# Causal attention in a decoder kernel: sums by quads of key tiles, a staggered search, and rows kept on chip

## What is computed

```python
scores = jnp.einsum('bhqd,bhkd->bhqk', q, k) * scale
scores = jnp.where(causal, scores, jnp.finfo(jnp.float32).min)
ex = jnp.exp(scores - jnp.max(scores, axis=-1, keepdims=True))
attn = ex / (jnp.sum(ex, axis=-1, keepdims=True) + 1e-08)
o = jnp.einsum('bhqk,bhkd->bhqd', attn, v)
out = jnp.einsum('bsi,oi->bso', o.transpose(0, 2, 1, 3).reshape(B, S, D), w_out) + b_out
```

## Time and profile before

| what | value |
|---|---|
| median of 3 runs | 9607.21 us (9586.43 to 9630.57) |
| profiled execution | 9610.03 us, its span 9608.2 us |
| PE busy | 7068.8 us, 74% of the span |
| DVE busy | 6895.6 us, 72% |
| ACT busy | 4456.8 us, 46% |
| POOL busy | 3936.4 us, 41% |
| mean granted PE clock | 0.748 of full speed |

### The profile page before, as it was taken

How to read it: one execution, slowest core, us unless ns; L and a number is a source line. 1 busy time by engine, 2 the same in 40 slices (tenths; PEclk the granted TensorE clock), 3 DMA queues, 4 the chain that set the end, 5 groups by cost and what they waited for, 6 DMA issues and landing times. The chain is left out here.

```text
span 9608.2 us, 163672 instructions
## 1 busy us (share of the span) xinstructions
PE 7068.8 (74%) x30924; PEld 2767.1 (29%) x30924; DVE 6895.6 (72%) x47725; ACT 4456.8 (46%) x8379; POOL 3936.4 (41%) x2613
## 2 busy tenths in 40 slices
PE   6888557666667656899766766656656789999983
PEld 2222222222222223555322222222223322222222
DVE  2655279999999997455399999999998343343423
ACT  1444246666666554111266767657656422222220
POOL 1000035555555443122155556545555045555550
PEclk7889656666666655799766677766766899999986
DMA  1000200000000000000100000000000311111103
GB/s 58 25 22 19 39 15 7 5 7 8 5 8 5 8 4 2 20 20 13 36 5 5 9 5 9 5 8 5 9 5 3 145 33 39 31 28 39 31 21 79
DMA packets 85686, 201.67 MB, mean 21 GB/s; under 512 B 25264, under 2 KB 39598, under 8 KB 80814
## 3 DMA queue, kind: packets, MB, share of 16 engines
q1 hardware_dynamic: 73390, 174.17, 6.6%
q10 hardware_dynamic: 11264, 16.79, 0.7%
HBM read 123.17 MB, written 66.95 MB: 20 GB/s over the span
## 5 line engine op out<-in xcount | busy, mean ns | idle before, releaser
L2100 DVE TENSOR_REDUCE l1xc_part_max<-l1xc_by_query 128x1 f32<-128x512 f32 (+1 forms) x1024 | 558.1, 571 | 875.6 <-PE l1xc_by_query L1959 856.1
L582 PE MATMUL l1ac_by_query<-l1ac_k_stack,l1ac_q_stack 97*128 (+1 forms) x1024 | 440.6, 496 | 831.4 <-ACT keep_xT L677 477.5
L770 DVE MAX8 l1ac_cand<-l1ac_score 128x8 f32<-128x32 f32 x8192 | 970.2, 192 | 27.9 <-ACT l1ac_score L677 16.7
L2058 ACT ACTIVATE l1xc_prob<-l1xc_less_max 128x512 f32<-128x512 f32 (+1 forms) x832 | 451.5, 594 | 1125.9 <-PE l1xc_less_max L1973 985.2
L770 DVE MAX8 l1ac_cand<-keep_xT 128x8 f32<-128x32 f32 x8192 | 962.6, 188 | 4.4
L582 PE MATMUL l0xc_by_query<-l0xc_k_stack,l0xc_q_stack 97*128 (+2 forms) x1024 | 385.8, 447 | 751.1 <-ACT keep_xT L677 492.4
L770 DVE MAX8 l0xc_cand<-l0xc_score 128x8 f32<-128x25 f32 (+1 forms) x8192 | 901.4, 180 | 27.4 <-ACT l0xc_score L677 15.8
L552 POOL TENSOR_SCALAR l1ac_lost<-l1ac_score,l1ac_tops 128x2048 bf16<-128x2048 f32 x128 | 696.0, 5437 | 512.5 <-DVE l1ac_tops L789 512.5
L770 DVE MAX8 l0xc_cand<-keep_xT 128x8 f32<-128x25 f32 (+1 forms) x8192 | 902.1, 180 | 4.4
L1921 POOL TENSOR_TENSOR l1xc_total<-l1xc_total,l1xc_prob 128x2048 f32<-128x2048 f32 (+1 forms) x176 | 794.0, 4511 | 72.2 <-POOL l1xc_v_tile L1931 71.9
L552 POOL TENSOR_SCALAR l1ac_lost<-keep_xT,l1ac_tops 128x2048 bf16<-128x2048 f32 x128 | 696.3, 5440 | 271.5 <-DVE l1ac_tops L789 271.5
(11 more groups left out here) (461 smaller groups left out, 14987.6 us busy)
## 6 DMA issues: line engine op xcount, KB each, us to landing
l1xc_k<-wide_k SPq DMA_DIRECT2D x32, 400.2 KB, 5.2
moe_w<-in_L_ffn_mlp_w_dram SPq DMA_DIRECT2D x16, 512.0 KB, 4.0
wide_q<-l1xp_full SPq DMA_DIRECT2D x8, 1024.0 KB, 3.9
wide_q_parts<-l1xp_parts SPq DMA_DIRECT2D x16, 512.0 KB, 5.6
l1xc_q_hm<-wide_q_parts SPq DMA_DIRECT2D x32, 256.0 KB, 3.8
l1xc_q<-wide_q SPq DMA_DIRECT2D x32, 256.0 KB, 5.7
wide_sums<-l1xc_o_out ACTq DMA_DIRECT2D x64, 128.0 KB, 2.3
l1xf_num<-wide_sums SPq DMA_DIRECT2D x16, 512.0 KB, 11.3
```

The costliest lines, as they stand in the source:

```text
L582: nc.tensor.matmul(sA[c % 2][:, 0:w], Qm[0:SHIFT_ROW, bass.ds(at + i * P, P)], Kb[0:SHIFT_ROW, bass.ds(at + a, w)], start=True, stop=True) ...
L770: seg = nc.vector.max(new[:, j:8 * NSEG:NSEG], score[i % 4][:, a:a + w])
L2058: nc.scalar.activation(prob[0:n, buf(j), c], yP[c % 2][0:n], ACT.Exp).then_inc(y_taken, 1)
L2100: nc.vector.tensor_reduce(part_max[:, i % 2, c:c + 1], a_bank(i, c)[:, 0:w], AX.X, ALU.max).then_inc(a_taken, 1)
```

## The change

- `attend_causal` is rewritten after the pattern of `attend_top`. Both the search and the products are flat lists of 40 pieces (`SEARCH`, `UNITS`). The products go by query chunk c, and within it by quads of four key tiles k up to the diagonal, 10 quads a head.
- At step u of head h the PE issues product piece u of head h and search piece u + 14 of head h + 1 (from u = 26 on, pieces of head h + 2). Ahead of the first head there are 54 steps of search alone; the last 54 product pieces have no search beside them.
- The sums of a quad are four matmuls into the four column groups of a bank, one per key tile, issued at step 4q + 6. There are two banks of sums; for it the search has 3 banks (4 before).
- When a query chunk is complete (4 times a head), ACT copies its bank, PE combines it by four f32 matmuls with `pick`, and ACT copies 68 columns into `O_all`. The zeroing matmul (L1279) remains once a head. The DMAs of the sums are gone.
- The maxima are copied by DVE into `stat_head`, split by POOL, turned by one bf16 matmul at step 29, copied by ACT, and sent by SP as three DMAs.
- v has no ones; POOL stages 4 tiles with one copy, 10 times a head, and the ones column is set once.
- POOL no longer clears the key stack, `stat`, `o_out` and `part_max`; the first loads wait for the two sets of rows only.
- `finish` and `load_head` are removed; `finish_rows` is called with the added 1e-8.

```diff
-def project(nc, G, A, tag, srcT, nk, wq, wk, wv, bq, bk, bv, rope, mask, V, ones=True):
+def project(nc, G, A, tag, srcT, nk, wq, wk, wv, bq, bk, bv, rope, mask, V):
...
-def attend_causal(nc, G, tag, V):
+def attend_causal(nc, G, tag, V, O_all):
+    UNITS = [(c, k, j) for c in range(QC) for k in range(c + 1) for j in range(4 * k, 4 * k + 4)]
+    SEARCH = [(i, c) for i in range(QT) for c in range(i // 4 + 1)]
+    QUADS = [(c, k) for c in range(QC) for k in range(c + 1)]
+    NU, NQ = len(UNITS), len(QUADS)
+    EARLY = 14
+    DV = DH + 1
...
-        A_AHEAD, Y_AHEAD, PV_AHEAD, O_AHEAD, M_AHEAD = 4, 2, 2, 1, 1
-        READY = 6
-        LAG = 4
+        A_AHEAD, Y_AHEAD, PV_AHEAD, O_AHEAD = 3, 2, 2, 2
+        READY, PARTS = 5, 5
...
+        def turns(eng, step, finish):
+            for u in range(NU + EARLY):
+                step(None, (u // NU, u % NU), -1, False)
+            step_all(step, 0, False)
+            with eng.Fori(1, H - 2) as h:
+                step_all(step, h, True)
+            step_all(step, H - 2, True)
+            step_all(step, H - 1, True)
+            finish()
+        def step_all(step, h, follows):
+            for u in range(NU):
+                a = (h + 1, u + EARLY) if u + EARLY < NU else (h + 2, u + EARLY - NU)
+                step(h, None if isinstance(h, int) and a[0] >= H else a, u, follows)
...
+            def sums(h, q):
+                c, k = QUADS[q]
+                hold(pe, (staged, NQ * h + q + 1), (y_taken, NU * h + 4 * q + 4 + Y_AHEAD))
+                if k == 0:
+                    hold(pe, (o_taken, QC * h + c - 2 + 1 + O_AHEAD))
...
+                for t in range(4):
+                    a = first_query(4 * k + t, c)
+                    mm = nc.tensor.matmul(O[c % 2][32 * t:32 * (t + 1), a:CH], Vh[:, q % 2, t],
+                                          prob[:, q % 2, t, a:CH], start=(k == 0 and c > 0), stop=(k == c),
+                                          skip_group_check=True)
                 mm.then_inc(pv_done, 1)
+            def combine(h, c, turned_heads):
+                g = QC * h + c
+                hold(pe, (o_taken, g + 1 + O_AHEAD), (comb_taken, g + 1), (st_out, turned_heads))
+                for t in range(4):
+                    mm = nc.tensor.matmul(turned[:, COMB_AT + t * DV:COMB_AT + (t + 1) * DV],
+                                          O_sb[:, c % 2, t * P:(t + 1) * P], pick[:], start=True, stop=True)
+                mm.then_inc(comb_formed, 1)
+            def turn(h, combined):
+                hold(pe, (parted, PARTS * (h + 1)), (st_out, h), (comb_taken, combined + 1))
...
+            def step(hb, a, u, follows):
                 if hb is not None:
+                    by_key(hb, u)
+                if a is not None:
+                    by_query(*a)
...
+                x = sums_at(hb, u, follows)
+                if x:
+                    sums(*x)
+                if u == NU - EARLY + 3 and not (isinstance(hb, int) and hb + 1 >= H):
+                    turn(hb + 1, QC * hb + 2)
...
+            def take_sums(h, q):
...
+                nc.scalar.activation(O_sb[:, c % 2], O[c % 2][:], ACT.Copy).then_inc(o_taken, 1)
+            def take_combined(h, q):
...
+                hold(act, (comb_formed, QC * h + c + 1))
...
-            attend_causal(nc, G, "l0ac", V)
-        row = lambda name: A[name].rearrange("(o n) -> o n", o=1)
-        finish(nc, G, A, "l0af", A["L0_attn_w_out"], row("L0_attn_b_out"), 1e-8)
+            attend_causal(nc, G, "l0ac", V, O_all)
+            finish_rows(nc, G, A, "l0af", A["L0_attn_w_out"], row("L0_attn_b_out"), O_all, 1e-8)
```

More of the change, by code:

```diff
@@ L921, in _ @@
                                         inv[:, at].unsqueeze(3).to_broadcast([P, 4, H, DH]), ALU.mult).then_inc(normed, 1)
[L922 to L970, removed]
-            act.wait_ge(turned, 1)
-            nc.scalar.activation(wT[:], banks[0][:].rearrange("p (c d) -> p c d", c=KC), ACT.Copy).then_inc(w_ready, 1)
-        @block.vector
-        def _(dve):
-            dve.wait_ge(loaded, LOADS)
-            k = 0
-            for c in range(KC):
-                if den_eps:
-                    nc.vector.tensor_scalar(den[:, c], den[:, c], den_eps, None, ALU.add).then_inc(normed, 1)
-                    k += 1
-                    dve.wait_ge(normed, k)
-                nc.vector.reciprocal(den[:, c], den[:, c]).then_inc(normed, 1)
-                k += 1
-                dve.wait_ge(normed, k)
-                nc.vector.tensor_tensor(num[:, c], num[:, c], den[:, c], ALU.mult).then_inc(normed, 1)
-                k += 1
@@ L1212, in _ @@
+            def step(hb, a, u, follows):
+                if hb is not None and u % 4 == 0:
+                    stage_v(hb, u // 4)
+                if a is not None and a[1] == NU - 1:
+                    part_max_rows(a[0])
+            turns(pool, step, lambda: None)
         @block.tensor
@@ L1295, in _, with finish @@
+            def finish():
+                sums(H - 1, NQ - 1)
+                combine(H - 1, QC - 1, H)
+            turns(pe, step, finish)
         @block.scalar
@@ L1298, in _ @@
             act.sem_inc(o_taken, O_AHEAD)
[L1299 removed]
+            act.sem_inc(comb_taken, 1)
             act.wait_ge(ready, READY)
[L1302 to L1310 removed]
@@ new lines, in step @@
+            def step(hb, a, u, follows):
+                if hb is None:
+                    if a == (1, 3):
+                        turn(0)
+                    return
+                weigh(hb, u)
+                x = sums_at(hb, u, follows)
+                if x and chunk_end(x[1]):
+                    take_sums(*x)
+                if u == NU - EARLY + 3 and not (isinstance(hb, int) and hb + 1 >= H):
+                    turn(hb + 1)
+                x = combine_at(hb, u, follows)
+                if x and chunk_end(x[1]):
+                    take_combined(*x)
@@ L1324, in _, with finish @@
+            def finish():
+                take_sums(H - 1, NQ - 1)
+                take_combined(H - 1, NQ - 1)
+            turns(act, step, finish)
         @block.vector
@@ L1366 @@
+            turns(dve, step, lambda: None)
 EXPERTS = 8
```

379 lines of the change are left out of this document (163 added, 216 removed).

## The result

The changed kernel takes 9343.36 us (median of 4 runs, 9320.69 to 9368.94) against 9610.42 for the kernel before in runs beside it (4 runs, 9586.43 to 9630.57): a ratio of 0.9724, 95% interval 0.969 to 0.9758. The forecast was 9388. The profiled executions are 9610.03 and 9320.69 us, with spans of 9608.2 and 9318.9, so the traces have 289.3 us to explain where the prediction's sum had 219.

| stage | before | after | less |
|---|---|---|---|
| start to the first search piece | 239.5 | 228.6 | 10.9 |
| causal attention with its finish | 883.9 | 689.2 | 194.7 |
| narrow cross attention | 2734.6 | 2704.5 | 30.1 |
| experts | 762.1 | 761.8 | 0.3 |
| narrow self attention | 2845.9 | 2798.1 | 47.8 |

A forecast was written before the change was run, and what follows sets the result against it. PE was taken to bound the body of a head, a chain PE, DVE, SP, DMA its edges. Gains of 161 and 58, sum 219 us, took 9610.0 to 9391; the median, 2.8 lower, was forecast at 9388, range 9320 to 9480.

The forecast's parts named there:

- the edge: Between two heads, the 3.5 us wait for the maxima's DMA goes; rival that it stays: 9440 us, 4%.
- the finish: End of the causal attention: 121.2 us becomes 62.9 as in the other stage, 0.5 added for the 1e-8; gain 58 us.
- A head, forecast 35.4: One turn of the causal loop over heads: ten quads at 31.4 us, four combines 3.5, and 0.5 more.
- A quad: In a head, 8 pieces at 0.26 us and one set of sums at 1.06: 3.14 us, ten of them 31.4.
- The term of 0.5: Per head, 0.5 us for the turn of the maxima, the zeroing and the loop's branch, also counting PE's stand.
- The combines: Four a head on PE, priced from another stage at 0.88 us each, 3.5 together.
- The 0.26: PE's us per piece with masks and gaps, from the old 2.61 us step less 1.06 for sums, over six pieces.
- the rival by which the engines take turns: At chunk ends PE and ACT wait for each other: 5.6 us more a head, 41 in all, 9470 us; 22%.
- DVE as the bound: Rival in the loop: DVE, not PE, sets the pace, a head 30.3 us, the time 9313 us; 12%.
- The clock: PE at 2.4 GHz throughout the loop, save once at the first products, which costs 5 us.
- the last rival: PE falls to 1.2 GHz in the loop and does not come back: 9851 us if always slow; 3%.
- The end of the stage: Causal attention before its finish ends at 841 us, where it ended at 1002.15; gain 161 us.

The follow-up runs named there:

- the kernel with 20 steps: The changed kernel with the search 20 pieces ahead of the products instead of 14: 9359.53 us, a head 37.47 us.
- the kernel with 3, 3 and 1 banks: The changed kernel with 3 banks for search, 3 for products, 1 for sums, instead of 3, 2, 2: median 9302.05 us, ratio 0.9661 to the kernel before.
- the pair without repairs: The kernel before and the changed kernel, both with the data-dependent second search of flagged query tiles never taken: 9477.66 and 9294.9 us.

## Why the prediction was right or wrong

**Right, in direction and in the place.** PE was the bound in the body of a head, and the edge with its half clock the other cost. Both went as described: the wait for the maxima's DMA is gone, the clock over the loop is 1.00 where I asked for 0.97, a head of 36.6 is within 34 to 37, sums of four take 1.06, the start is at 228.57 (229.0 forecast) and the finish takes 62.9 us (63.4 with the added 1e-8). That the finish takes just this is in part luck: the trace of before has `finish_rows` twice, at 62.8 us and, in the self attention, at 37.3 (from 7428.7 on), and the forecast took the first. By the other it would have been 26 us lower.

**A head, forecast 35.4, measured 36.60.** In the head around the rows above, the ten distances from one set of sums to the next (493.63 to 530.53) are 4.11, 3.93, 3.30, 4.19, 4.02, 3.56, 4.02, 3.29, 3.19 and 3.29 us. The first, second, fourth and seventh hold a combine of 0.91, the fifth the stand of 0.91 for DVE, the sixth the turn, the last the zeroing. Together they are 36.90, 1.5 more than forecast, and three terms share it:

- A quad was to take 8 x 0.26 + 1.06 = 3.14 and takes 3.2 on the mean, ten of them about 0.6 more.
- The term of 0.5 for the turn, the zeroing and the branch was too small by about 0.8. The forecast had spent it on these three and then counted the stand of 0.5 to 1 us in it as well. The stand is 0.91, and I estimate the three at 0.4 (two matmuls of 0.2, the branch hidden).
- The combines cost 0.1 more than forecast.

The 0.26 came from a step of 3 and 3 pieces with two product banks, so it held waits for ACT already, and they are still there in the new order (50.4 us of weight-load wait in 300). With the third product bank they mostly go: of the ten distances of a head (515.34 to 549.74) eight are then 2.7 to 3.0 us less their combine or stand, and a head is 2.3 us shorter.

So the rival by which the engines take turns was half right. PE does wait for ACT with two product banks, and the sign named for it, ACT waiting over 1 us at each copy of the sums, is there (1.1 us). But its place was wrong. The four distances in which ACT copies a bank (the first, third, sixth and last) take 3.1 to 3.4 us less combine, turn and zeroing, and those without copy and combine 3.1 to 3.3 less the stand; so PE loses little more at the chunks' ends than elsewhere. And the third product bank leaves ACT's wait at the copies as it is and still brings the 2.3. Its size, 5.6 us a head, was too large; a head came out 1.2 above the forecast.

**The combine** was forecast at 0.88 and is 0.91. By the rule of the Trainium skill, page "TensorEngine Tiling (Array Packing)", section "Instruction Overhead", it would have been about 0.2 (an estimate from that page); the trace disagrees, by the 0.91 and by the 3.6 us that four more of them a head cost at full clock.

**DVE as the bound** is excluded: half its work in the maxima brings 0.5 us a head. The warning of the Trainium skill, page "TensorEngine Tiling (Array Packing)", section "PSUM Bottleneck", that the reader of the results may be next, did not come true for DVE here; ACT as reader of the product banks is the case nearest to it, with 2.3 us.

**The edge.** I expected a stand of 0.5 to 1 us at the turn. It is 0.91, not at the turn but before it, at the last search piece, for DVE; the turn itself comes 0.65 us after POOL is ready. The wait for the maxima's DMA comes back when the stagger is cut to 4 steps.

**The clock.** 5 us were set aside for the first products; the stretch from 270 to 808 has 1.00 on the mean, so that was too much. That the clock would hold through short stands was borne out in this kernel, with its 0.91 us once a head. It is not a rule to count on: the kernel with 20 steps has stands of 0.82 us and falls to half clock in half of its heads. Nor does PE always come back, as the last rival has it from the loop: in the finish of the kernel before that begins at 3795, PE is busy 55.06 of the 56 us from 3801 to 3857 at a granted clock of 0.50.

**The end of the stage.** Forecast 841; the finish's reciprocal starts at 854.9. The head explains 14.65 x 1.2 = 18 us, less the 5 of the clock: 13 of the 14.

**The sum.** Start and stage 205.6 us against 219, right to 6%. What was wrong is the sentence "Nothing else in the program is touched". The code of the other stages is untouched; their data are not, to the last bits (as argued above), and a branch on the data stands in two of them. The forecast had nothing for it, and was 84 us too high by what lies outside the causal attention, 71 of them two repairs fewer. The two errors go opposite ways, 13 and 84: the forecast for the profiled execution was 9391, and it came out at 9320.7. The median lies 23 us higher than that execution, which is why the forecast of the median misses by 45 only. That is luck. The profiled execution lies 0.7 us inside the lower end of the range, whose reason was DVE's floor, which is not where the time came from; without the 84 us the median would have been near 9427, 39 above the forecast.

## What to carry to other kernels

A wait of 4 us at the edge of the loop cost twice on PE, by itself and through the half clock after it; moving the producer ahead by ten steps removed both (5.5 us a head, 42.1 to 36.6). The f32 matmuls of the sums, 32 columns of weights each, cost by the set and not by the matmul (1.05 us for one and for four), so fill all four column groups; then look which bank PE waits for before dealing the banks out, for the second bank of sums was not missed and a third product bank brought 2.3 us a head. Before writing that a stage is untouched, look for branches on data in it and count how often the trace of before takes them.

## What the runs showed of the hardware that I had not expected

`finish_rows` takes 62.9 us or 37.2 us for the same instructions. Measured from its reciprocal to the layer norm over the 40 times that it stands in the 14 profiles, it took 62.7 to 63.0 us 23 times, 37.2 or 37.3 nine times, and between 41 and 55 eight times. It is the granted clock. Busy time by stretch, the kernel after and then the kernel with 3, 3 and 1 banks in the execution of the table above (columns as in the earlier trace rows):

```profile
854.00:856.00 2.00, 0.00 (x0) 0.00 (x0) 1.47 (x2) 0.00 (x0) 0.00 (x0) 0.50 0.16 44
856.00:858.00 2.00, 0.03 (x1) 0.03 (x1) 1.97 (x3) 0.00 (x0) 0.00 (x0) 0.50 0.31 100
858.00:862.00 4.00, 3.31 (x13) 2.89 (x14) 3.33 (x3) 1.79 (x3) 0.00 (x0) 0.50 0.00 0
862.00:880.00 18.00, 18.00 (x41) 10.44 (x40) 2.12 (x5) 1.19 (x2) 0.00 (x0) 0.50 0.00 0
880.00:900.00 20.00, 20.00 (x47) 11.30 (x46) 2.12 (x5) 1.79 (x3) 0.00 (x0) 0.50 0.00 0
900.00:917.00 17.00, 16.48 (x34) 9.01 (x34) 2.55 (x6) 0.60 (x1) 0.00 (x0) 0.50 0.00 0
```

```profile
818.00:820.00 2.00, 0.00 (x0) 0.00 (x0) 1.88 (x2) 0.00 (x0) 0.00 (x0) 0.50 0.43 100
820.00:822.00 2.00, 0.43 (x2) 0.43 (x3) 1.97 (x3) 0.00 (x0) 0.00 (x0) 0.50 0.13 41
822.00:826.00 4.00, 3.31 (x16) 2.67 (x14) 2.92 (x3) 1.79 (x3) 0.00 (x0) 0.67 0.00 2
826.00:840.00 14.00, 14.00 (x59) 8.53 (x59) 3.12 (x8) 1.79 (x3) 0.00 (x0) 1.00 0.00 0
840.00:854.00 14.00, 14.00 (x59) 8.61 (x58) 3.25 (x8) 1.79 (x3) 0.00 (x0) 1.00 0.00 0
```

PE stands 4.6 us before each, until 857.97 and 821.57. In the one it then stays at 1.2 GHz, though it is busy 54.5 of the 55 us from 862 to 917; in the other it is at 2.4 GHz from 825 on, less than 4 us after it starts again. I found no difference in the work before that would tell them apart, and leave the cause open. What it means for reading such profiles is plain: 25.6 us of a finish, 0.27% of the time, come or go with it. In the main comparison the self attention's finish is a fast one in both kernels, and the new causal one is slow. It is more than the 23.4 us by which the self attention of the pair without repairs differs (37.3 and 62.9), and it makes 26 of the 64 us by which the causal attention with its finish was shorter in that execution with 3, 3 and 1 banks. For the differences of single profiles, the time of a head is a safer measure than the span.
